# A four-layer graph network on Trainium2: edge rows are sent to their places in other stages, and each half of a step of the last layer owns a source tile

## What is computed

```python
x = _layernorm(x + _L0_gnn_ref(x, ...))   # two GIN convolutions: segment_sum(x[src], dst), two matmuls
x = _layernorm(x + _L1_gnn_ref(x, ...))   # two attention convolutions over the edges
x = _layernorm(x + _L2_gnn_ref(x, ...))   # four blocks: graph convolution, then GRU gates
x = _layernorm(x + _L3_gnn_ref(x, edge_attr_64, src, dst, ...))
```

```python
W = jax.nn.silu(rbf_ij @ W1 + b1) @ W2 + b2     # one filter per edge, from its 64 attributes
msgs = h[idx_j] * W                             # idx_j is dst
agg = jnp.zeros(...).at[idx_i].add(msgs)        # idx_i is src: the edges are not sorted by it
delta = jax.nn.silu(agg @ W3 + b3) @ W4 + b4
```

## Time and profile before

| | |
|---|---|
| median of 3 runs | 6668.77 us (6667.44 to 6669.37) |
| profiled execution, its own time | 6675.19 us |
| its span | 6673.6 us |
| instructions | 101944 |
| busy: PE, DVE, POOL | 4334.3 us (65%), 3767.7 us (56%), 3659.2 us (55%) |
| granted PE clock, mean | 0.833 |
| indirect DMAs issued by POOL | 784 sends, 1792 gathers of attention, 880 of the last layer |

### The profile page before, as it was taken

One profiled execution on the slowest core, in us unless ns is written; L12 is line 12 of the kernel. 1 busy time (PEld: TensorE's weight loads), 2 busy tenths in 40 slices (PEclk: granted clock), 3 DMA queues, 4 the chain that ended last, 5 costly groups with the idle time before them and its releaser, 6 DMA issues. The chain is left out here.

```text
span 6673.6 us, 101944 instructions
## 1 busy us (share of the span) xinstructions
PE 4334.3 (65%) x26966; PEld 3026.4 (45%) x26967; DVE 3767.7 (56%) x8412; ACT 1205.4 (18%) x2011; POOL 3659.2 (55%) x3721
## 2 busy tenths in 40 slices
PE   0666667186267777775466666641888778778774
PEld 0111114154156566553355555531555556556653
DVE  8777771054589898988466666662111244444443
ACT  0111111011211111111212211110211222222221
POOL 1666664600277777772477777735000057777771
PEclk9999998598589899987577777766998888888886
DMA  4111114110244444443233333353000123222344
GB/s 198 41 44 44 41 44 177 46 33 15 64 127 116 123 122 121 117 123 75 74 81 80 79 80 83 82 114 130 11 18 21 31 64 75 74 75 74 75 71 42
DMA packets 309188, 518.20 MB, mean 78 GB/s; under 512 B 105621, under 2 KB 221727, under 8 KB 298934
## 3 DMA queue, kind: packets, MB, share of 16 engines
q0 software_dynamic: 131616, 291.86, 18.6%
q1 hardware_dynamic: 177430, 224.82, 10.3%
HBM read 412.95 MB, written 103.45 MB: 77 GB/s over the span
## 5 line engine op out<-in xcount | busy, mean ns | idle before, releaser
L1017 POOL DMA_INDIRECT e_ring<-att_rows,e_near x1792 | 1841.6, 1028 | 550.2 <-issue 484.2
L1770 POOL DMA_INDIRECT e_nodes<-x,e_edges x880 | 884.2, 1005 | 311.5 <-issue 274.5
L1084 PE MATMUL e_psum<-e_ring,e_whole_pick 128*128 128x264 f32 (+1 forms) x3584 | 849.5, 390 | 297.8 <-DVE e_ring L1244 288.8
L1084 PEld LDWEIGHTS e_psum<-e_ring,e_whole_pick 128*128 128x128 f32 x3584 | 649.4, 225 | 423.5 <-issue 195.7
L1039 PE MATMUL e_px<-t_parts,e_pick 128*128 x5376 | 692.9, 270 | 118.1 <-DVE e_prod L1162 56.3
L1162 DVE TENSOR_TENSOR e_prod<-e_px,e_ring 128x512 f32<-128x512 f32 x672 | 458.3, 682 | 495.9 <-DMA e_ring<-att_rows,e_near 413.3
L1688 POOL DMA_INDIRECT sorted<-bx_held,bx_index x550 | 545.0, 991 | 251.3 <-issue 248.9
L280 PE MATMUL b_acc<-b_pick_key,b_pick_lo 128*128 128x416 bf16 (+1 forms) x1960 | 504.4, 346 | 176.5 <-DVE b_pick_key L251 159.5
L350 PE MATMUL r_pa<-gru_counts,gru_parts 128*128 x3000 | 448.7, 316 | 187.3 <-DMA r_bh<-in_gru_bh 169.6
L1039 PEld LDWEIGHTS e_px<-t_parts,e_pick 128*128 128x128 bf16 x5376 | 452.6, 107 | 210.2 <-issue 139.5
L1126 ACT ACTIVATE e_whole_pick<-e_pturn 128x512 f32<-128x512 bf16 x448 | 266.5, 595 | 1324.8 <-PE e_pturn L1075 1280.5
(11 more groups left out here) (335 smaller groups left out, 6579.9 us busy)
## 6 DMA issues: line engine op xcount, KB each, us to landing
e_relb<-place SPq DMA_DIRECT2D x56, 1024.0 KB
sorted<-o_fill SPq DMA_DIRECT2D x13, 2244.0 KB, 34.3
e_edges<-sorted SPq DMA_DIRECT2D x221, 132.0 KB
e_ring<-att_rows,e_near POOLq DMA_INDIRECT x1792
kept<-gin_counts SPq DMA_DIRECT2D x5, 4000.0 KB, 33.5
gru_counts<-kept SPq DMA_DIRECT2D x5, 4000.0 KB
bx_held<-in_edge_rows POOLq DMA_DIRECT2D x51, 363.0 KB
e_nodes<-x,e_edges POOLq DMA_INDIRECT x880
```

Source lines behind the costliest of these rows:

```text
L1017: pool.indirect_dma_start(out=ring[:, s, r, 0:wd + HEADS], out_offset=None, in_=xrows, in_offset=bass.IndirectOffsetOnAxis(ap=near[:, s, r ...
L1084: mm = pe.matmul(psum[q % 2][:, 0:RING], whole_pick[:, q % 2, c, :], ring[:, s, q * G + c, :], start=(c == 0), stop=(c == G - 1))
L1770: pool.indirect_dma_start(out=nodes[:, s, u, :], out_offset=None, in_=source, in_offset=bass.IndirectOffsetOnAxis(ap=edges[:, q, u, RBF + ...
```

## The change

The group of 512 rows becomes two halves of EHALF = 256 rows, and each half belongs to one source tile. The padding is then at most 255 rows per tile instead of 511, and NGRP falls from 220 to 208. A step still takes 512 rows in four sub-tiles: a pair of sub-tiles is a half. PE's four matmuls go into two PSUM areas, DVE reads two tile numbers and adds twice, with a drain behind each.

The 782 sends (the two spare chunks are gone) are dealt out anew: `build_counts` 168 (24 batches of 7), first `gin_conv` 150 (10 batches of 15), `edge_tables` 32 (2 batches of 16), `softmax_norm` none, and each of the four `gru_block` stages 108 (12 batches of 9). To make room in SBUF for the senders' buffers, `work` in `gru_block` shrinks from five slots to three, with `reset` in the place of `summed` and `cand` in that of `conv`.

```diff
+                sender.send(pool, 0, 0, first=True)
+                add_own(0)
+                with pool.Fori(0, NT // 2 - 1) as j:
+                    sender.send(pool, j, 1)
+                    add_own(j * 2 + 1)
+                    sender.send(pool, j + 1, 0)
+                    add_own(j * 2 + 2)
+                sender.send(pool, NT // 2 - 1, 1)
+                add_own(NT - 2)
+                add_own(NT - 1)
...
@@ edge_tables, POOL
                 pool.memset(src[:, ECH:WIDE], 0).then_inc(ready, 1)
+                sender.begin(pool)
+                sender.send(pool, 0, 0, first=True)
+                sender.send(pool, 0, 1)
+                sender.end(pool)
...
@@ softmax_norm
-            @block.gpsimd
-            def _(pool):
-                sender.run(pool)
...
@@ gru_block
-        work = m.sb("r_work", [P, NG, GW])
-        summed, conv, reset, keep, cand = (work[:, i, :] for i in range(NG))
-        split = Split(m, source, 1, parts, [work[:, i, :].rearrange("p (t c) -> p t c", c=P) for i in range(NG)], from_scale)
+        work = m.sb("r_work", [P, 3, GW])
+        summed = reset = work[:, 0, :]
+        conv = cand = work[:, 1, :]
+        keep = work[:, 2, :]
+        split = Split(m, source, 1, parts, [work[:, i, :].rearrange("p (t c) -> p t c", c=P) for i in range(3)], from_scale)
+        sender = Sender(m, D, "r", *GRU_SENDS[b])
...
+            @block.gpsimd
+            def _(pool):
+                sender.run(pool)
...
-NGRP = (EP + NT * (EGRP - 1)) // EGRP
+HALVES = 2
+EHALF = EGRP // HALVES
+NGRP = -(-((EP + NT * (EHALF - 1)) // EHALF) // HALVES)
+NHALF = NGRP * HALVES
...
-COUNT_SENDS = (0, 11, NT)
-GIN_SENDS = (2 * 11 * NT, 5, 15)
-GRU_SENDS = (2 * (11 * NT + 75), 6, 7)
+COUNT_SENDS = (0, 7, NT - 1)
+GIN_SENDS = (7 * (NT - 1), 15, 10)
+TABLE_SENDS = (7 * (NT - 1) + 150, 16, 2)
+GRU_SENDS = [(7 * (NT - 1) + 182 + 108 * b, 9, 12) for b in range(4)]
...
@@ edge_order
-        count = m.sb("o_count", [P, NGRP])
-        tile = m.sb("o_tile", [P, NGRP])
+        count = m.sb("o_count", [P, NHALF])
+        tile = m.sb("o_tile", [P, NHALF])
...
@@ edge_messages, SP
-                    sp.dma_start(edges[:, q, :, :], D["sorted"][ds(n * EGRP, EGRP), :].rearrange("(p u) w -> p u w", u=SUB)
+                    sp.dma_start(edges[:, q, :, :].rearrange("p (h u) w -> p h u w", h=HALVES),
+                                 D["sorted"][ds(n * EGRP, EGRP), :].rearrange("(h p u) w -> p h u w", h=HALVES, p=P)
...
@@ edge_messages, PE
-                        mm = pe.matmul(pa[s][:, 0:P], pick[:, s, u, :], msg[:, s, u, :], start=(u == 0), stop=(u == SUB - 1))
+                        part = u // (SUB // HALVES)
+                        mm = pe.matmul(pa[s][:, part * P:(part + 1) * P], pick[:, s, u, :], msg[:, s, u, :],
+                                       start=(u % (SUB // HALVES) == 0), stop=(u % (SUB // HALVES) == SUB // HALVES - 1))
...
@@ edge_messages, DVE
-                    t = dve.value_load(src_tile[0:1, ds(g, 1)], min_val=0, max_val=NT - 1)
-                    part = agg[:, ds(t, 1), :].rearrange("p o f -> p (o f)")
+                    tiles = [dve.value_load(src_tile[0:1, ds(g * HALVES + h, 1)], min_val=0, max_val=NT - 1)
+                             for h in range(HALVES)]
                     dve.wait_ge(sums, g + 2)
-                    dve.tensor_tensor(part, part, pa[s][:, 0:P], ALU.add).then_inc(added, 1)
+                    for h, t in enumerate(tiles):
+                        part = agg[:, ds(t, 1), :].rearrange("p o f -> p (o f)")
+                        dve.tensor_tensor(part, part, pa[s][:, h * P:(h + 1) * P], ALU.add)
+                        dve.drain()
+                    dve.sem_inc(added, 1)
```

More of the change, by code:

```diff
@@ L204, in _, with add_own @@
                 sender.begin(pool)
-                def tile(t, first):
-                    sender.send(pool, t, 0, first)
-                    sender.send(pool, t, 1)
+                def add_own(t):
                     pool.wait_ge(moved, t * (2 * PER) + 2 * PER + 2)
@@ L211, in tile @@
                     pool.tensor_tensor(block_, block_, K["identb"][:, :], ALU.add).then_inc(diag, 1)
-                tile(0, True)
-                with pool.Fori(1, NT) as t:
-                    tile(t, False)
+                sender.send(pool, 0, 0, first=True)
[8 more added lines that the diff above has]
+                add_own(NT - 1)
                 pool.wait_ge(diag, NT)
@@ L541, in edge_tables @@
         bound = m.sb("p_bound", [1, NT + 1])
+        sender = Sender(m, D, "p", *TABLE_SENDS)
         boundi = m.sb("p_boundi", [1, NT + 1], I32)
@@ L1314, in softmax_norm @@
         ones = m.sb("u_ones", [P, P], BF16)
-        sender = Sender(m, D, "u", *GRU_SENDS)
         psum = [m.ps(f"u_psum{q}", [P, BANK]) for q in range(Q)]
@@ L1573, in _ @@
                 sp.wait_ge(filled, 2)
-                table = D["sorted"][0:(NGRP + 1) * EGRP, :].rearrange("(p n r) w -> n p r w", n=13, r=FILL)
-                for n in range(13):
+                table = D["sorted"].rearrange("(p n r) w -> n p r w", n=11, r=FILL)
+                for n in range(11):
                     sp.dma_start(table[n], fill[:, :, :]).then_inc(blank, 16)
@@ L1593, in _ @@
                 pool.memset(every[:, :], 1.0)
-                pool.iota(count[:, :], pattern=[[1, NGRP]], base=0, channel_multiplier=0,
-                          allow_small_or_imprecise_dtypes=True)
-                pool.iota(spare[:, :], pattern=[[P, NSC - NC]], base=(NGRP + 1) * EGRP, channel_multiplier=1,
+                pool.iota(count[:, :], pattern=[[1, NHALF]], base=0, channel_multiplier=0,
                           allow_small_or_imprecise_dtypes=True).then_inc(ready, 1)
@@ L1625, in _ @@
                 dve.drain()
-                dve.scalar_tensor_tensor(out=offset[:, :], in0=first[:, :], scalar=float(EGRP), in1=ppast[:, 0:NT],
+                dve.scalar_tensor_tensor(out=offset[:, :], in0=first[:, :], scalar=float(EHALF), in1=ppast[:, 0:NT],
                                          op0=ALU.mult, op1=ALU.add)
@@ L1640, in _ @@
                 dve.tensor_scalar(tile_base[:, :], tile[:, :], float(P), None, ALU.mult)
-                dve.tensor_copy(src_tile[0:1, 1:NGRP + 1], tile[0:1, :])
-                dve.tensor_copy(slot[:, NC:NSC], spare[:, :])
+                dve.tensor_copy(src_tile[0:1, HALVES:NHALF + HALVES], tile[0:1, :])
                 dve.drain()
-                dve.tensor_copy(slot[:, 0:NC], slotf[:, :])
+                dve.tensor_copy(slot[:, :], slotf[:, :])
                 dve.drain().then_inc(listed, 1)
@@ L1655, with __init__ @@
 class Sender:
-    def __init__(self, m, D, tag, first, size, pairs):
-        self.D, self.first, self.size, self.pairs = D, first, size, pairs
-        self.slot = m.sb(f"{tag}x_slot", [P, 2 * pairs * size], I32)
+    def __init__(self, m, D, tag, first, size, batches):
+        self.D, self.first, self.size, self.batches = D, first, size, batches
+        self.slot = m.sb(f"{tag}x_slot", [P, batches * size], I32)
         self.index = [m.sb(f"{tag}x_index{s}", [P, size], I32) for s in range(2)]
@@ L1673, in begin @@
     def begin(self, pool):
-        pool.dma_start(self.slot[:, :], self.D["slot"][:, ds(self.first, 2 * self.pairs * self.size)]).then_inc(self.listed, 16)
+        pool.dma_start(self.slot[:, :], self.D["slot"][:, ds(self.first, self.batches * self.size)]).then_inc(self.listed, 16)
         self.load(pool, 0, 0)
@@ L1694, in run @@
         self.send(pool, 0, 0, first=True)
-        self.send(pool, 0, 1)
-        with pool.Fori(1, self.pairs) as j:
-            for s in range(2):
-                self.send(pool, j, s)
+        with pool.Fori(0, self.batches // 2 - 1) as j:
+            self.send(pool, j, 1)
+            self.send(pool, j + 1, 0)
+        self.send(pool, self.batches // 2 - 1, 1)
         self.end(pool)
     def end(self, pool):
-        pool.wait_ge(self.sent[0], self.pairs * self.size * 16)
-        pool.wait_ge(self.sent[1], self.pairs * self.size * 16)
-        pool.wait_ge(self.loaded[0], self.pairs * 16 + 16)
+        n, full = self.batches, self.size * 16
+        for s in range(2):
+            pool.wait_ge(self.sent[s], (n + 1 - s) // 2 * full)
+        pool.wait_ge(self.loaded[n % 2], n // 2 * 16 + 16)
 def edge_messages(nc, K, D, source, agg):
@@ L1876, in _ @@
                         add(g, (q + 1) % 2)
-                t = dve.value_load(src_tile[0:1, NGRP:NGRP + 1], min_val=0, max_val=NT - 1)
-                part = agg[:, ds(t, 1), :].rearrange("p o f -> p (o f)")
-                dve.wait_ge(sums, NGRP + 2)
-                dve.drain()
-                dve.tensor_tensor(part, part, pa[(NGRP + 1) % 2][:, 0:P], ALU.add)
-                dve.drain()
+                add(NGRP, (NGRP + 1) % 2)
 def node_update(nc, K, D, source, agg, target):
```

38 lines of the change are left out of this document (20 added, 18 removed).

## The result

The changed kernel takes 6451.37 us (median of 4 runs, 6444.01 to 6452.62), the kernel before 6669.07 beside it: a ratio of 0.9669, 95% interval [0.9656, 0.9682]. That is 217.7 us less; the forecast was 201 less, and 6467 in a range of 6436 to 6516. The profiled spans are 6673.6 and 6451.0 us. The total came out within 17 us, in part by luck, since errors of its terms cancel: the last layer gave 97 us instead of 64, and the other terms together 11 us less than forecast (126 by the spans, 137 in the sum).

The account below looks back on a forecast made before the run. POOL's sends were taken to play a part in four places and its gathers to set the last layer's step. Terms 5 - 35 - 63 + 2 - 82 + 36 - 64 = -201 from median 6668.8 gave about 6467 us, range 6436 to 6516.

Parts of the forecast that it names:

- Edge order, table and softmax stage: Three stages: longer scans +5 us, sends mostly hidden behind DVE +2, POOL's sends gone from the softmax end -82.
- Count stage, -35: Count stage 35 us shorter: POOL's late end -13.6, and DVE less slowed by sends, 21 us.
- With 382 / 550 of the sends gone 21 us go: Count stage: sends slow DVE's compares by 30.4 us, all on the path; fewer sends remove 21 us.
- First GIN layer, -63: First GIN layer: 10 batches of sends instead of 30, -84 us when steady, less 21 us for stalls during the matrix write.
- GRU blocks, +36: Four GRU blocks: weights queue behind waiting loads, +8.0 us per block, plus 1 per block for slowed DVE.
- Rival 1: GRU blocks: POOL becomes the bound if each batch loses 1.7 us, 11.5 us more per block, 6513 us; chance 0.15.
- Last layer, -64: Last layer: 12 fewer steps save 65 us, DVE's new work hides in its wait, the last addition costs 1.
- 12 steps fewer at 5.418 us are -65: Last layer: each dropped step was priced at the mean step of 5.418 us, 65 us in all.
- an unchanged 5.42 us: Last layer: step length stays 5.42 us while DVE's wait for gathered rows falls from 1.80 to about 0.35 us.
- Rival 2: Last layer: DVE becomes the bound if its added work exceeds 1.80 us per step; at 2.2 us, 6551 us; chance 0.10.
- The rule weighed: Skill's rule that DVE and GpSimd lock each other out of a shared port; count stage's 550 sends taken as against it.
- rival 3: Table stage and GRU blocks: sends and DVE hold each other, 6 us and 70 us for four blocks, 6543 us; chance 0.05.

Follow-up runs that it names:

- experiment 8: Kernel before with only the halves (two tiles of 256 rows per step, 208 steps), sends unmoved, on a faster chip: 6587.11 us, ratio 0.9871.
- Experiment 4: Changed kernel with the count matrix written to DRAM in the second GIN layer instead of the first, on a slower chip: ratio 0.96 to the kernel before.
- experiment 6: Changed kernel with the weights' transfers ahead of the last two piece loads in each GRU block: 6444.78 us, ratio 0.966 to the kernel before.

## Why the prediction was right, and where it was not

- *Edge order, table and softmax stage:* +5.8, +0.7 and -80.0 against +5, +2 and -82. The terms hold; the 24 scans give 4.9 of the 5.8 us.
- *Count stage, -35:* the POOL tail gave -15.3 (forecast -13.6). "With 382 / 550 of the sends gone 21 us go" gave -13.2 at most, since experiment 8 has an end 7.7 us earlier with every send in place. DVE did get some 20 us faster; that all of this is on the path was too much. Why the rest did not reach the end, no run shows.
- *First GIN layer, -63:* the sends took 29 us more than their steady 216, and not 21. Experiment 4 puts 24 of them down to the matrix write; the other 5 are in the batches themselves. I had scaled the stalls by the number of batch borders, but fewer borders met longer ones. Still the stage came within its bounds (-84 to -50).
- *GRU blocks, +36:* the mechanism held, PE at 15.7 to 17.1 us instead of 17.7, by the weights behind the waiting loads. The blocks grew by 6.7 us on average and not 9: the start is 6.4 us later on average and not 8.0, and the 1 us for slower DVE did not show. That POOL is done just before is right too; experiment 6 puts its bound at 181, where I had 179.7. Rival 1 was added up wrongly: 12 batches at 1.7 us more are 20.4, which is 16 past the bound and not 11.5, so its time would be 6531 and lie outside the range.
- *Last layer, -64:* the term that failed is "12 steps fewer at 5.418 us are -65". The mean of 220 steps stood for two kinds. Seven of the 12 dropped steps were filler steps at 6.98 us and five were steps with edges at 5.316: -48.9 and -26.6, so -75.4 instead of -65. And "an unchanged 5.42 us" failed as well: the 202 intervals left between steps with edges are each 0.113 us shorter, another -22.8. Together that is -98, and the layer gave -96.6. The shortening comes of fewer long gathers: their excess fell by 0.255 - 0.145 = 0.11 us per step, and what is left of a step is 5.06 us before and after. Rival 2 was rightly put low: DVE's added work fitted into its wait, of which 0.16 us per step is left.
- *The rule weighed.* I took the earlier trace rows as speaking against the Trainium skill (SBUF — State Buffer, Who interferes with whom), and this was wrong. By that section a DVE instruction with two SBUF inputs contends with a GpSimd instruction that reads SBUF, one with at most one SBUF input outside the two-port modes does not, and whoever issues first blocks the other for the whole instruction. In the last layer the trace agrees in one direction: a gather that begins behind the start of a two-input operation waits for its end, one that begins beside an addition from PSUM does not. In the other direction it does not: in the kernel before 246 two-input operations began inside a running gather and took 691 to 717 ns, with the median of all (693), and 245 of these gathers were not long. The section also reports a probe in which a two-input operation did not stall a DMA; here such operations do hold its issue. The sends of the count stage, which I judged by, stand beside compares with a single source, and even of the 297 that began beside the wide one 46 took over 1.024 us (at most 1.182). And gathers were held in the kernel before, where I had the mean of 1005 ns against a median of 944 before me and did not ask for the 61 ns, 54 us in the layer. What I had right is its small size for the sends: in the four GRU blocks 22 of the 24 sends that begin beside the split's operations on two SBUF inputs (L337, L341, L345) take 1.13 to 1.63 us, 8 us more in all, not rival 3's 70.

## What to carry to other kernels

Before multiplying a mean step by a number of steps removed, look at the last steps by themselves: padding may cost more than work, above all where all its gathers name the same row. Work on a side engine is priced by the stage it stands in (1.2 us or 0.01 us for the same send), so fill stages that another engine ends first, and check that price on a second chip (1.16 us there). Where a mean is above its median, look at what the other engine does at the start of the long ones. And when one bound of a stage is lifted, the gain is the distance to the next one: 2.4 us of 7 here.

## What the runs showed that was not expected

- 128 lanes gathering one row keep the DMA engines busy for 0.93 to 0.95 of the time at 56 to 59 GB/s; different rows, 0.20 at 58 GB/s.
- A POOL gather that begins while DVE runs an operation on two SBUF inputs starts its 0.82 us when that ends (499 of 499 long gathers in four profiles), and one that begins beside an operation on PSUM takes its usual 0.94. A two-input operation that begins inside a gather holds neither.
- A batch border of POOL's sends (copy, drain and wait) costs 2.3 to 2.7 us, and up to 17.5 while a large matrix is being written.
- Chips differ by 15% on the kernel before. On the slower ones the steps of the last layer take 6.7 us instead of 5.2 to 5.3, with median gathers as short (944 to 947 ns), and a count stage with 168 sends takes the same 856 us on both kinds.
